# Ten norm stages of a hybrid transformer kernel, moved into the stages that use them

## The chip, the cores and the metric
The kernel runs on one core of a Trainium2 chip. The metric is the device time in microseconds of one execution: 2873.79 us, the median of three runs (2870.31 to 2880.94).

## The reference
Eight sub-layers, each of the form x = x + f(layernorm(x)), on x of [4, 256, 256] float32, which is 1024 tokens of 256 features. In order: linear attention, mixture of experts (8 experts, top 2), convolution with a scan, the same mixture of experts, softmax attention, a block "L1_ffn" of softmax attention and a routed FFN, delta-rule attention, and the L1_ffn block again.

```python
def _layernorm(x, axis=-1, eps=1e-05):
    m = jnp.mean(x, axis=axis, keepdims=True)
    v = jnp.var(x, axis=axis, keepdims=True)
    return (x - m) / jnp.sqrt(v + eps)
```

Some sub-layers put an RMS norm on top, x * rsqrt(mean(x*x) + eps) * weight: linear attention (eps 1.19e-7, no weight), convolution (1e-6, norm_scale) and the first half of L1_ffn (1e-6, w_ln1). The second half of L1_ffn starts with an RMS norm alone (w_ln2), on the residual inside the block. Convolution and L1_ffn keep the layer-normed x as their own residual, so it is added to the output besides x.

## The kernel before
Everything is hand-scheduled. X and XN are SBUF tensors of 128 partitions x 8 tiles x 256 features (token-major), XT is 128 x 2 x 1024 (feature-major, what the projections need). PS is the PSUM, eight banks of 512 float32. A `Stage` takes semaphores from a pool of 80 and opens SBUF tensors; inside an `nc.Block()` each engine has its own program, and order between engines is by semaphores alone. `Stage.end` clears the stage's semaphores on GpSimd and puts a barrier over all engines, after which the next stage starts with everything at zero. `Chain.then` makes an engine wait for its own last instruction.

`norm` (L163 to L258) is such a stage. VectorE does bn_stats on eight tiles, then bn_aggr on eight (mean and variance), ACT the square root (L236), VectorE the reciprocal (L200) and eight scalings (L202) of X into XN. With an RMS norm on top, VectorE works out its mean square from variance and rstd (L209, L210), ACT takes a second root (L239), VectorE a reciprocal (L218) and eight scalings into H (L220). Only when all eight tiles are scaled does TensorE transpose them (L255, 16 transposes into four banks); VectorE copies the banks of the first 128 features to XT (L227 or L230), ACT those of the second (L244 or L247), with the weight multiplied in where there is one. With `layer=False` (twice, ahead of the routed FFN) there is only the RMS norm, of XN.

`program` calls it ten times, each right ahead of the stage that needs XT: linear_attention (L261), moe (L404, twice), conv_scan (L694), softmax_attention (L926, three times), routed_ffn (L1285, twice) and delta_attention (L1574). In these stages SP issues the weight loads first; with the start of a stage TensorE waits for them. Beside that, at the start of a stage:
- moe: ACT copies XN twice into the row buffer XW (L591, L592), VectorE sets constants, TensorE runs the router (L513), 16 matmuls of 8 columns.
- conv_scan: GpSimd sets constants (L757 to L762), copies half heads of the weights when they have landed (L767, L768) and adds XN to X (L770). VectorE clips XT into XP (L775) and does four taps of a causal convolution in two halves (L786 and six of L788), then ACT takes the SiLU and TensorE starts (L904). VectorE goes on to the head_mix products KM (L797), which are wanted much later.
- softmax_attention: GpSimd sets V's zeros (L1011), the causal masks (L1012 to L1018), in the form with RoPE it swaps half heads (L1027, L1028), in the plain form it adds the output bias to X (L1032). VectorE makes a small table (L1207, L1209), ACT warms up Exp (L1152).
- routed_ffn: ACT rounds XT to XP (L1480), VectorE takes the remainder (L1538), TensorE runs the router (L1418).
- delta_attention: SP spills X and loads eleven sets of constants (L1645 to L1655), GpSimd sets six buffers, the last S with 8192 elements per partition (L1666), VectorE reorders XT into XB (L1686) and XP (L1690), TensorE multiplies XB (L1674), a barrier follows, then the loop over four blocks.

Of the kernel before, what the change touches and what calls it, by code (L numbers as in the profile page):

```python
# [10 lines left out]
ALU = mybir.AluOpType  # L11
# [151 lines left out]
def norm(core, layer=True, rms_eps=None, weight=None):  # L163


    nc, X, XN, XT, PS = core.nc, core.X, core.XN, core.XT, core.PS
    s = Stage(core, "norm")
    stats = s.sb("stats", [P, NT, 6])
    mv = s.sb("mv", [P, NT, 2])
    root = s.sb("root", [P, NT])  # L170
    rstd = s.sb("rstd", [P, NT])
    rms = s.sb("rms", [P, NT])
    eps = s.sb("eps", [P, 2])
    w = s.sb("w", [P, KD])
    H = s.sb("H", [P, NT, D]) if rms_eps is not None else XN
    w_in, sumsq, rooted, scaled, turned, moved, chain_v = (s.sem(n) for n in (
        "w_in", "sumsq", "rooted", "scaled", "turned", "moved", "chain_v"))
    src = X if layer else XN
    with nc.Block() as block:
        @block.sync  # L180
        def _(sp):
            if weight is not None:
                sp.dma_start(w[:], weight.rearrange("(k p) -> p k", p=P),
                             allow_slow_non_contiguous=True).then_inc(w_in, 16)
                sp.wait_ge(w_in, 16)

        @block.vector
        def _(dve):
            c = Chain(dve, chain_v)
            nc.vector.memset(eps[:, 0:1], LN_EPS)  # L190
            c.then(nc.vector.memset(eps[:, 1:2], rms_eps or 0.0))
            for i in range(NT):
                last = nc.vector.bn_stats(stats[:, i, :], src[:, i, :])
            c.then(last)
            for i in range(NT):
                last = nc.vector.bn_aggr(mv[:, i, :], stats[:, i, :])
            if layer:
                last.then_inc(sumsq, 1)
                dve.wait_ge(rooted, 1)
                c.then(nc.vector.reciprocal(rstd[:], root[:]))  # L200
                for i in range(NT):
                    last = nc.vector.tensor_scalar(XN[:, i, :], X[:, i, :], mv[:, i, 0:1], rstd[:, i:i + 1],  # L202
                                                   ALU.subtract, ALU.mult)
# [18 lines left out]
            for q in range(2):  # L222
                dve.wait_ge(turned, q + 1)
                if weight is not None:
                    if q == 0:
                        dve.wait_ge(w_in, 16)
# [2344 lines left out]
```

## Time and profile before

| what | us |
|---|---|
| median of three runs | 2873.79 |
| profiled execution, whole | 2874.2 |
| its span | 2872.4 |
| TensorE busy (matmuls) | 2101.9 (73%) |
| VectorE busy | 1594.2 (55%) |
| GpSimd busy | 1183.2 (41%) |
| ACT busy | 1119.7 (39%) |
| mean granted TensorE clock, of full speed | 0.817 |
| the transposes L255, per norm | 3.64 to 3.68 |
| router matmuls L513, 95.95 to 102.95 | 7.0 |
| last instruction before to first after a barrier: 79.41 to 80.07 (12 semaphores), 91.28 to 91.88 (7), 390.34 to 391.06 (24), 740.94 to 741.70 (30) | 0.66, 0.60, 0.72, 0.76 |
| GpSimd's opening work in plain attention, 605.76 to 610.16 | 4.4 |
| plain attention: transposes end 604.6, L1051 starts 608.6; granted clock 608.6 to 611.7 | 0.50 |
| first rotated key for ACT in attention with RoPE: 760.22 to 775.05 | 14.8 |

No engine is busy all the time, so a busy share alone says little here: the program is a row of stages, and in each another chain sets the length. Times in the rows below count from the start of the span. TensorE's matmul records are called PE, its weight loads PEld, VectorE DVE, GpSimd POOL, SyncE's DMA queue SPq.

### The profile page before, as it was taken

To read this page: it belongs to the slowest core of one execution; us is meant where nothing else is said; L and a number is where in the kernel's file an instruction comes from. 1 tells how busy PE (TensorE), PEld (TensorE's weight loads), DVE (VectorE), ACT (ScalarE), POOL (GpSimd) and SP (SyncE) were. 2 spreads that over 40 slices of the span, in tenths; PEclk is the share of its full clock that TensorE was granted. 3 is DMA by queue.
4 is the path that set the end of the run, shared out by engine and by line. 5 is a ranking of instruction groups with operands and counts; after the bars stand their busy time and mean duration, and the time that the engine had idled before them with its cause. 6 is when DMAs were issued, how large, how long until landed. Compare 5 with 4: busy or idle time off the path is not lost. (4 is left out here: it accounts for less than half of the span.)

```text
span 2872.4 us, 41835 instructions
## 1 busy us (share of the span) xinstructions
PE 2101.9 (73%) x15312; PEld 1628.4 (57%) x15312; DVE 1594.2 (55%) x3209; ACT 1119.7 (39%) x2681; POOL 1183.2 (41%) x999
## 2 busy tenths in 40 slices
PE   6398438958776995856797577965789667668698
PEld 4264224635354784746687466854667656435486
DVE  1322752234554334786876967867677678354433
ACT  2111221125254332743465444643446434215433
POOL 0222112210000652696736965378643869100154
PEclk9599668979898996967699586976779676879799
DMA  7232003210001502331323322233222422100250
GB/s 242 97 63 37 19 28 74 22 39 1 21 1 40 180 0 57 112 120 62 125 75 101 116 74 97 92 105 108 88 70 79 122 89 89 58 25 1 65 154 15
DMA packets 137424, 212.91 MB, mean 74 GB/s; under 512 B 61184, under 2 KB 113680, under 8 KB 132112
## 3 DMA queue, kind: packets, MB, share of 16 engines
q1 hardware_dynamic: 129072, 200.11, 21.7%
q0 software_dynamic: 8160, 10.26, 2.3%
q8 instruction: 118, 1.93, 0.3%
q14 instruction: 74, 0.61, 0.1%
HBM read 187.97 MB, written 22.37 MB: 73 GB/s over the span
## 5 line engine op out<-in xcount | busy, mean ns | idle before, releaser
L1977 PE MATMUL PS<-ident,XT 128*128 128x128 f32 x512 | 114.2, 405 | 251.6 <-DVE XT L2349 237.8
L2291 DVE SCALAR_TENSOR_TENSOR XT<-M_delta,CW_delta,XT 128x256 f32<-128x256 f32 x576 | 249.8, 494 | 71.4 <-ACT M_delta L2160 41.7
L1926 PE MATMUL PS<-XP_delta,X 128*128 128x268 f32 (+1 forms) x1024 | 241.4, 388 | 6.7 <-DMA X<-in_L_attn_b_heads 6.6
L1977 PEld LDWEIGHTS PS<-ident,XT 128*128 128x128 f32 x512 | 91.3, 209 | 271.1 <-DVE XT L2349 132.4
L1926 PEld LDWEIGHTS PS<-XP_delta,X 128*128 128x128 f32 x1024 | 192.9, 189 | 56.4 <-issue 11.9
L1439 PE MATMUL PS<-XP_rffn,UW_rffn 128*128 128x512 f32 x816 | 195.1, 396 | 5.8 <-POOL UW_rffn L1395 4.6
L1395 POOL TENSOR_TENSOR UW_rffn<-W_rffn,UW_rffn 128x512 fp32r<-128x512 f32 x34 | 44.2, 1299 | 347.4 <-ACT UW_rffn L1498 347.4
L1865 POOL TENSOR_TENSOR DD_delta<-DD_delta,A_delta 128x64 f32<-128x64 f32 (+6 forms) x224 | 170.0, 759 | 39.2 <-ACT A_delta L2248 19.5
L1439 PEld LDWEIGHTS PS<-XP_rffn,UW_rffn 128*128 128x128 f32 x816 | 155.9, 192 | 39.8 <-issue 7.1
L1891 POOL TENSOR_TENSOR M_delta<-M_delta,DD_delta 128x2304 f32<-128x2304 f32 x32 | 165.0, 5157 | 0.0
L505 POOL DMA_INDIRECT sums<-XS_moe,token_moe x46 | 71.7, 1559 | 219.0 <-ACT XS_moe L601 200.0
L1990 PEld LDWEIGHTS PS<-XN,KQ_delta 16*128 16x128 f32 (+2 forms) x3072 | 148.7, 295 | 7.3 <-issue 7.3
L2262 ACT ACTIVATE S_delta<-S_delta,AO_delta 128x128 f32<-128x128 f32 x512 | 152.1, 390 | 0.0
L1251 DVE TENSOR_REDUCE NM_attn<-PS 128x4 f32<-128x512 f32 (+1 forms) x144 | 92.1, 682 | 107.0 <-PE PS L1077 107.0
L1990 PE MATMUL PS<-XN,KQ_delta 16*128 16x16 f32 (+2 forms) x3072 | 151.3, 345 | 0.0
L1558 DVE TENSOR_TENSOR SU_rffn<-PS,CB_rffn 128x512 f32<-128x512 f32 x68 | 47.0, 691 | 181.3 <-PE PS L1439 158.6
L1957 PE MATMUL PS<-KQ_delta,TR_delta 128*128 128x64 f32 x1024 | 136.4, 280 | 14.6 <-DVE TR_delta L2308 14.5
L2240 ACT COPY KQ_delta<-PS 128x512 f32<-128x512 f32 x128 | 73.2, 584 | 179.0 <-PE PS L1977 179.0
L1957 PEld LDWEIGHTS PS<-KQ_delta,TR_delta 128*128 128x128 f32 x1024 | 131.3, 201 | 18.9 <-DVE TR_delta L2308 18.9
L1404 POOL TENSOR_TENSOR HP_rffn<-HF_rffn,HP_rffn 128x512 fp32r<-128x512 f32 x68 | 92.5, 1380 | 116.8 <-ACT HP_rffn L1521 116.8
L1175 ACT ACTIVATE PR_attn<-PS,NM_attn 128x256 f32<-128x256 f32 (+1 forms) x384 | 129.1, 466 | 28.1 <-DVE NM_attn L1251 28.1
L1807 POOL TENSOR_SCALAR XT<-M_delta,CW_delta,CB_delta 128x256 f32<-128x256 f32 x64 | 51.7, 808 | 163.1 <-ACT M_delta L2160 163.1
(359 smaller groups left out, 5038.6 us busy)
## 6 DMA issues: line engine op xcount, KB each, us to landing
M_delta<-gram_delta SPq DMA_DIRECT2D x32, 2304.0 KB, 8.8
X<-in_L_attn_b_heads SPq DMA_DIRECT2D x64, 512.0 KB, 3.2
EW<-in_L_ffn_w SPq DMA_DIRECT2D x24, 512.0 KB, 9.1
CB_rffn<-routes_rffn SPq DMA_DIRECT2D x20, 512.0 KB, 23.2
XN<-in_L_attn_b_outs SPq DMA_DIRECT2D x16, 512.0 KB, 3.6
F_delta<-in_L_attn_b_outs SPq DMA_DIRECT2D x4, 2048.0 KB, 8.2
W_rffn<-in_L_ffn_tiles SPq DMA_DIRECT2D x4, 1536.0 KB, 11.5
slots<-pad SPq DMA_DIRECT2D x2, 2967.0 KB, 14.5
```

The costliest lines, as they stand in the source:

```text
L1175: last = nc.scalar.activation(PR[:, u % (2 * ROWS), j * w:(j + 1) * w], PS[:, r, j * w:(j + 1) * w], ACT.Exp, bias=NM[:, u % (2 * ROWS), j ...
L1251: nc.vector.tensor_reduce(NM[:, u % (2 * ROWS), 0:per], PS[:, r, :].rearrange("p (h j) -> p h j", h=per), AX.X, ALU.max, negate=True).then ...
L1404: nc.gpsimd.tensor_tensor(HP[1][:, r, x], HF[:, n, :], HP[0][:, r, x], ALU.subtract).then_inc(hl_d, 1)
L1439: last = nc.tensor.matmul(PS[:, 4 + 2 * n + q, :], UW[qw][:, r, (q * KD + k) * P:(q * KD + k + 1) * P], XP[qx][:, k, n * NB:(n + 1) * NB], ...
L1865: last = nc.gpsimd.tensor_tensor(DD[:, :, tri(t - 1) + 1:tri(t)], DD[:, :, tri(t):tri(t + 1)], step(t).broadcast_to([P, BH, C - t]), ALU.mult)
L1891: nc.gpsimd.tensor_tensor(q, q, by_h(DD[:]), ALU.mult).then_inc(mq_d, 1)
L1926: last = nc.tensor.matmul(PS[:, 1 + i, 0:B * (WIN - halo)], WH[:, r, i, k, :], XP[:, k, :, n * BT + halo:n * BT + WIN], start=(k == 0), st ...
L1957: last = nc.tensor.matmul(PS[:, 5 * (g % 2), i * 2 * OC:(i + 1) * 2 * OC].rearrange("p (q t) -> p q t", q=2), TR[:, g % 3, i * P:(i + 1) * ...
L1977: last = nc.tensor.transpose(PS[:, 6 + r % 2, i * P:(i + 1) * P], W[:, B * h:B * (h + 1), :], core.ident[:])
L1990: last = nc.tensor.matmul(PS[:, 1 + b, h * 2 * C:(h + 1) * 2 * C].rearrange("p (q t) -> p q t", q=2), WT(o)[rows, h, :], GR[rows, o, h].re ...
L2262: last = nc.scalar.activation(S[:, lane, :], S[:, lane, :], ACT.Copy, scale=AO[:, lane:lane + 1])
L2291: nc.vector.scalar_tensor_tensor(TMP[:, r, i], RAW[:, r, i, :, tau:tau + BT], CW[:, i, h, tau:tau + 1], TMP[:, r, i], ALU.mult, ALU.add).t ...
```

## The change
The function `norm` goes. A class `Norm` takes its place; it has one method for each engine, which writes the norm's instructions at the head of that engine's program in the stage that uses it, with the stage's own semaphores. There is no barrier between norm and stage. `ready` and `rows_ready` are waits for XT and for the scaled rows, put where the stage reads them. SP's loads of the stage, GpSimd's opening work and the norm run beside each other.

Within the norm the tokens go in two halves of four tiles for the statistics, roots and scale factors. Even tiles are scaled by VectorE, odd ones by ACT (Identity with scale and shift, the shift being -mean * scale). The RMS norm's scale is 1/sqrt((1 + eps2) var + eps1 eps2), straight from the variance, so there is one scaling only; the plain layer norm that conv_scan and L1_ffn need as residual is made by eight more activations on ACT after the norm (`residual`). TensorE transposes tile by tile as they come.

```diff
-def norm(core, layer=True, rms_eps=None, weight=None):   # the whole stage goes
+class Norm:
+    def ready(self, engine):
+        engine.wait_ge(self.moved_v, 2)
+        engine.wait_ge(self.moved_a, 2)
+
+    def rows_ready(self, engine):
+        engine.wait_ge(self.tile_v, NT // 2)
+        engine.wait_ge(self.tile_a, NT // 2)
...
+    def vector(self, dve):
+        nc, mv, XT, PS = self.core.nc, self.mv, self.core.XT, self.core.PS
+        c = Chain(dve, self.chain)
...
+        for q in range(2):
+            h = self.half(q)
+            for i in range(h.start, h.stop):
+                last = nc.vector.bn_stats(self.stats[:, i, :], self.src[:, i, :])
+            c.then(last)
+            for i in range(h.start, h.stop):
+                last = nc.vector.bn_aggr(mv[:, i, :], self.stats[:, i, :])
+            if self.layer:
+                last.then_inc(self.stat_d, 1)
...
+        for q in range(2):
+            h = self.half(q)
+            dve.wait_ge(self.root_d, q + 1)
+            if self.layer:
+                c.then(nc.vector.reciprocal(self.scale[:, 0:1 + self.use, h], self.root[:, 0:1 + self.use, h]))
+                u = 1 + self.use
+                nc.vector.scalar_tensor_tensor(self.shift[:, 0:u, h], mv[:, h, 0].unsqueeze(1).broadcast_to([P, u, NT // 2]), -1.0,
+                                               self.scale[:, 0:u, h], ALU.mult, ALU.mult).then_inc(self.scale_d, 1)
...
+            for i in range(h.start, h.stop, 2):
+                if self.layer:
+                    nc.vector.tensor_scalar(self.H[:, i, :], self.src[:, i, :], mv[:, i, 0:1],
+                                            self.scale[:, self.use, i:i + 1], ALU.subtract,
+                                            ALU.mult).then_inc(self.tile_v, 1)
...
+        for q in range(2):
+            dve.wait_ge(self.turned, 2 * q + 1)
...
+                nc.vector.tensor_copy(XT[:, 0, q * NB:(q + 1) * NB], PS[:, q, :]).then_inc(self.moved_v, 1)
+
+    def scalar(self, act):
+        for q in range(2):
+            h = self.half(q)
+            act.wait_ge(self.stat_d, q + 1)
+            last = nc.scalar.activation(self.root[:, 0, h], mv[:, h, 1] if self.layer else self.square[:, h], ACT.Sqrt,
+                                        bias=self.eps[:, 0:1])
+            if self.use:
+                last = nc.scalar.activation(self.root[:, 1, h], mv[:, h, 1], ACT.Sqrt, bias=self.eps[:, 1:2],
+                                            scale=1.0 + self.rms_eps)
+            last.then_inc(self.root_d, 1)
+        for q in range(2):
+            h = self.half(q)
+            act.wait_ge(self.scale_d, q + 1)
+            for i in range(h.start + 1, h.stop, 2):
+                if self.layer:
+                    nc.scalar.activation(self.H[:, i, :], self.src[:, i, :], ACT.Identity, bias=self.shift[:, self.use, i:i + 1],
+                                         scale=self.scale[:, self.use, i:i + 1]).then_inc(self.tile_a, 1)
...
+    def tensor(self, pe):
+        for q in range(2):
+            h = self.half(q)
+            for i in range(h.start, h.stop):
+                if i % 2 == 0:
+                    pe.wait_ge(self.tile_v, i // 2 + 1)
+                else:
+                    pe.wait_ge(self.tile_a, i // 2 + 1)
+                for k in range(KD):
+                    last = nc.tensor.transpose(PS[:, 2 * k + q, (i - h.start) * P:(i - h.start + 1) * P],
+                                               self.H[:, i, k * P:(k + 1) * P], self.core.ident[:])
...
+    def residual(self, act):
+        for i in range(NT):
+            nc.scalar.activation(self.core.XN[:, i, :], self.src[:, i, :], ACT.Identity, bias=self.shift[:, 0, i:i + 1],
+                                 scale=self.scale[:, 0, i:i + 1]).then_inc(self.residual_d, 1)
```

In the stages (conv_scan shown; the others alike):

```diff
+    norm = Norm(core, s, rms_eps=1e-6, weight=a["L0_attn_b_norm_scale"],
+                hidden=GT[:].rearrange("p k n -> p (k n)").rearrange("p (i d) -> p i d", d=D))
         @block.sync
         def _(sp):
+            norm.sync(sp)
...
+            pool.wait_ge(norm.residual_d, NT)
             nc.gpsimd.tensor_tensor(X[:], X[:], XN[:], ALU.add).then_inc(res_d, 1)
         @block.vector
         def _(dve):
+            norm.vector(dve)
+            norm.ready(dve)
...
         @block.scalar
         def _(act):
+            norm.scalar(act)
+            norm.residual(act)
             act.wait_ge(c_in, 48)
...
         @block.tensor
         def _(pe):
+            norm.tensor(pe)
+            norm.ready(pe)
             pe.wait_ge(w_in, 64)
```

moe waits with `rows_ready` on ACT ahead of L591; routed_ffn with `ready` on ACT ahead of L1480; plain attention with `rows_ready` on GpSimd ahead of L1032; delta_attention with `ready` on VectorE ahead of L1686. With weights or a residual, H is laid over a buffer that the stage fills later (GT, PR or CB). `core.clear(6)` in delta_attention becomes the count of its semaphores; each stage has 11 more.

## Rows read from the trace of the kernel before

**Rows 1.** Windows: stretch, length, busy us of each engine, granted clock, DMA.
```profile
core 0: us, PE busy (x) PEld busy (x) DVE busy (x) ACT busy (x) POOL busy (x), PEclk, DMA share, GB/s
7.24:30.15 22.91, 3.68 (x17) 3.28 (x17) 10.34 (x38) 4.14 (x6) 0.00 (x0) 0.88 0.29 84
80.27:95.95 15.68, 3.67 (x17) 3.28 (x17) 8.74 (x66) 6.60 (x7) 0.97 (x5) 0.58 0.18 57
286.20:304.46 18.26, 3.67 (x16) 3.27 (x16) 13.36 (x39) 3.07 (x5) 3.20 (x6) 0.50 0.06 6
391.25:405.05 13.80, 3.68 (x16) 3.28 (x17) 8.74 (x66) 4.74 (x6) 0.97 (x5) 0.58 0.07 21
594.15:608.64 14.49, 3.68 (x17) 3.28 (x17) 9.37 (x29) 4.05 (x6) 2.82 (x3) 0.62 0.09 19
741.90:760.22 18.32, 3.64 (x16) 3.27 (x16) 12.20 (x40) 4.55 (x7) 3.38 (x5) 0.59 0.12 29
907.04:921.28 14.24, 3.68 (x17) 3.28 (x17) 8.43 (x38) 5.34 (x6) 0.00 (x0) 0.57 0.07 5
1089.32:1116.89 27.57, 3.68 (x16) 3.28 (x16) 19.48 (x32) 3.84 (x5) 11.24 (x6) 0.57 0.41 45
2519.66:2538.19 18.53, 3.67 (x16) 3.27 (x17) 12.21 (x40) 4.32 (x7) 3.57 (x5) 0.59 0.12 30
2688.36:2702.66 14.30, 3.68 (x16) 3.27 (x16) 8.48 (x38) 5.59 (x6) 0.00 (x0) 0.50 0.07 7
30.15:35.04 4.89, 4.89 (x6) 2.18 (x7) 0.00 (x0) 0.60 (x1) 0.00 (x0) 0.50 1.09 318
1125.00:2506.00 1381.00, 1018.31 (x9280) 882.37 (x9280) 1000.60 (x1916) 663.77 (x1716) 862.25 (x704) 0.77 0.28 93
```

**Rows 2.** Timeline, first norm: start, length, engine, line, instructions, idle before.
```profile
7.24 2.71 DVE L193 BATCH_NORM_STATS2 stats_norm<-X 128x6 f32<-128x256 f32 x8
...
10.66 0.30 ACT L236 ACTIVATE root_norm<-mv_norm,eps_norm 128x8 f32<-128x8 f32 x1 [2.34 <-DVE mv_norm L196]
...
11.23 2.67 DVE L202 TENSOR_SCALAR XN<-X,mv_norm,rstd_norm 128x256 f32<-128x256 f32 x8
...
17.16 3.67 PE L255 MATMUL PS<-ident,H_norm 128*128 128x128 f32 x16 [17.16 <-DVE H_norm L220]
...
20.87 0.58 ACT L247 COPY XT<-PS 128x512 f32<-128x512 f32 x1 [0.27 <-PE PS L255]
22.05 0.38 SPq L280 DMA_DIRECT2D W_linattn<-in_L_attn_a_Wq  x1
...
30.15 23.31 PE L291 MATMUL PS<-XT,W_linattn 128*128 128x512 f32 x48 [9.31 <-DMA W_linattn<-in_L_attn_a_Wp]
```

**Rows 3.** Groups of ACT instructions: busy, mean ns, idle before.
```profile
L601 ACT ACTIVATE XS_moe<-PS,XS_moe 128x256 f32<-128x256 f32 x46 | 21.8, 474 | 159.1 <-PE PS L570 159.1
...
L591 ACT COPY XW_moe<-XN 128x2048 f32<-128x2048 f32 x2 | 3.8, 1902 | 1.2 <-PEq L122 1.2
```

**Rows 4.** Timeline of the delta stage's opening.
```profile
1100.93 0.32 SPq L1645 DMA_DIRECT2D spill_delta<-X  x1
...
1104.70 7.46 POOL L1666 MEMSET S_delta<- 128x8192 f32 x1
```

**Rows 5.** Timeline of the convolution stage, VectorE, then GpSimd.
```profile
301.15 2.90 DVE L775 TENSOR_SCALAR XP_cscan<-XT 128x2048 f32<-128x2048 f32 x1 [2.27 <-PEq L122]
...
305.91 7.58 DVE L788 SCALAR_TENSOR_TENSOR A_cscan<-XP_cscan,CW_cscan,A_cscan 128x1024 f32<-128x1024 f32 x6
...
313.80 5.06 DVE L797 TENSOR_TENSOR KM_cscan<-HM_cscan,IM_cscan 128x256 f32<-128x256 f32 x2
...
301.17 1.80 POOL L758 MEMSET KEEP_cscan<- 128x2048 f32 x1
...
313.62 4.50 POOL L770 TENSOR_TENSOR X<-X,XN 128x2048 f32<-128x2048 f32 x1
```

**Rows 6.** Timeline of plain attention's opening, VectorE.
```profile
605.80 0.29 DVE L1207 TENSOR_REDUCE HALF_attn<-ident 128x2 f32<-128x128 f32 x1 [2.23 <-PEq L122]
```

More of the change, by code:

```diff
@@ L160, in finish @@
     s.end()
-def norm(core, layer=True, rms_eps=None, weight=None):
[L166 to L193, printed above, removed]
-            c.then(last)
[L195 to L203, printed above, removed]
-                if rms_eps is None:
-                    last.then_inc(scaled, 1)
-                else:
-                    c.then(last)
-                    c.then(nc.vector.tensor_tensor(rms[:], mv[:, :, 1], rstd[:], ALU.mult))
-                    nc.vector.tensor_tensor(rms[:], rms[:], rstd[:], ALU.mult).then_inc(sumsq, 1)
@@ L211, in _ @@
             else:
                 c.then(last)
-                c.then(nc.vector.tensor_tensor(rms[:], mv[:, :, 0], mv[:, :, 0], ALU.mult))
-                nc.vector.tensor_tensor(rms[:], rms[:], mv[:, :, 1], ALU.add).then_inc(sumsq, 1)
-            if rms_eps is not None:
-                dve.wait_ge(rooted, 1 + layer)
-                c.then(nc.vector.reciprocal(rms[:], root[:]))
-                for i in range(NT):
-                    last = nc.vector.tensor_scalar(H[:, i, :], XN[:, i, :], rms[:, i:i + 1], None, ALU.mult)
-                last.then_inc(scaled, 1)
@@ L249, in _ @@
-        @block.tensor
-        def _(pe):
-            pe.wait_ge(scaled, 1)
-            for k in range(KD):
-                for q in range(2):
-                    for i in range(4):
-                        last = nc.tensor.transpose(PS[:, 2 * k + q, i * P:(i + 1) * P],
-                                                   H[:, 4 * q + i, k * P:(k + 1) * P], core.ident[:])
-                    last.then_inc(turned, 1)
-    s.end()
+                c.then(nc.vector.tensor_tensor(self.square[:, h], mv[:, h, 0], mv[:, h, 0], ALU.mult))
@@ L509, in _ @@
         def _(pe):
+            norm.tensor(pe)
+            norm.ready(pe)
             pe.wait_ge(g_in, 16)
@@ L888, in _ @@
         def _(pe):
+            norm.tensor(pe)
+            norm.ready(pe)
             pe.wait_ge(w_in, 64)
@@ L1036, in _ @@
         def _(pe):
+            norm.tensor(pe)
+            norm.ready(pe)
             pe.wait_ge(q_in, QK_IN)
@@ L1328, in routed_ffn @@
         "up_mm", "silu_d", "su_d", "h_d", "dn_mm", "yt_ev", "y_mm"))
+    norm = Norm(core, s, layer=False, rms_eps=1e-6, weight=a["L1_ffn_w_ln2"],
+                hidden=CB[:, 0:2].rearrange("p m n -> p (m n)").rearrange("p (i d) -> p i d", d=D))
     PIECES = []
@@ L1414, in _ @@
         def _(pe):
+            norm.tensor(pe)
+            norm.ready(pe)
             pe.wait_ge(g_in, 32)
@@ L1479, in _ @@
         def _(act):
+            norm.scalar(act)
+            norm.ready(act)
             nc.scalar.copy(XP[0][:], XT[:]).then_inc(xh_d, 1)
@@ L1669, in _ @@
         def _(pe):
+            norm.tensor(pe)
+            norm.ready(pe)
             pe.wait_ge(c_in, CIN)
@@ L1684, in _ @@
         def _(dve):
+            norm.vector(dve)
+            norm.ready(dve)
             for k in range(KD):
```

116 lines of the change are left out of this document (83 added, 33 removed).

## The prediction
> **What bounds the kernel now.** I read the stretches between stages first, since the change lives only there. At ten places a norm stands as a stage of its own, closed by a barrier, and the stage behind it then starts its loads and waits for them. The windows table [rows 1] has one line for each place, cut from the norm's first bn_stats to the first instruction of the next stage that needs XT and a loaded operand (for the convolution stage: its first tap). The reader is to see that each stretch is 14 to 28 us long and that TensorE does one thing in it, the 16 transposes (3.6 to 3.7 us busy); the first ten lines add up to 178.1 us, 6.2% of the span. Nothing else of the program can run there, so whatever a stretch loses the whole time loses, as long as the stage behind it keeps its shape.
>
> The timeline of the first place [rows 2] shows what a stretch is made of: bn_stats of eight tiles 7.24 to 9.95, the square root on ACT at 10.66, eight scalings by VectorE 2.67, for norms followed by an RMS norm a second round until 17.16, transposes, and 20.87 + 0.58 = 21.45 the last copy. Only at 22.05 does SP issue the first weight load, and TensorE starts at 30.15, released by that DMA. The loads need none of the norm's results: 8.10 us of 22.9 are a wait that could lie beside the norm.
>
> **The new norm, step by step.** All times count from the first bn_stats, s. VectorE: bn_stats cost 2.71/8 = 0.34 each, so the first half ends at 1.42; the gap from the last bn_stats to the root (9.95 to 10.66) makes eight aggregations 0.7, so four 0.36. First half done 1.8, second 3.6. ACT takes the first root (0.30) beside the second half, the second at 3.64 to 3.94 (with an RMS norm two small activations, to 4.2: still before it is needed). VectorE reaches the reciprocal of the first half at 3.6, the shift at 3.83, and tile 0 at 3.9; a scaling is 2.67/8 = 0.33 apart with 0.4 for one, so tile 0 is ready at 4.3. ACT's tiles: the trace has no ACT scaling SBUF to SBUF of 256 elements. From below 1.90/8 = 0.24, an eighth of its 2048-element copy from SBUF [rows 3]; from above 0.474, a 256-element scaling with a pointer, though out of PSUM [rows 3]. I take the upper, as it has the size and the form: tile 1 at 4.5, tile 3 at 4.95. Second half: VectorE tiles 4 and 6 ready at 5.3 and 5.65, ACT's 5 and 7 at 5.5 and 6.0. TensorE needs 3.67/16 = 0.23 for a transpose [rows 2], so 16 of them from 4.35 on end later than every tile: it sets the end. From its start to the last copy's end it took 21.45 - 17.16 = 4.29 before, the last copy now behind the same sixteenth transpose. XT is whole at s + 8.65, +0.1 where a weight is multiplied in. Its ends: 7.9, with TensorE starting when the second half's statistics are there (3.6 + 4.29), and 14.2, the old chain. The second scaling round of the RMS norms is gone (its root comes from the variance), so these gain 5.6, the plain ones 2.35. In the two norms with layer=False the square and the sum stand in each half ahead of the root, four dependent small operations of 0.2: s + 9.4.
>
> **What waits behind it, place by place** (stretches from [rows 1]):
> - Linear attention, 22.91: loads issued at 7.04 instead of 22.05 land 8.10 later, at 15.1; XT is whole at 7.24 + 8.65 = 15.9. TensorE starts at 15.95: -14.2. The large loads of expert weights queue behind these on SP as before, only earlier.
> - MoE, 15.68 and 13.80: the router weights land within 4 us of issue and are there. Both start at s + 8.7: -7.0 and -5.1. ACT's two row copies, 3.8 us [rows 3], and a table load of 1.28 now start when TensorE starts the router; they used to start 4 us before it. The router matmuls take 7.0 us (table above), so they cover 5.1; with the cover gone it would cost up to 5 each. VectorE's memsets come behind the norm, 1.1 us, under the same cover.
> - Softmax attention, 14.49 (plain) and 18.32, 18.53 (RMS): s + 8.7 and s + 8.8, plus 0.3 for GpSimd (below): -5.5, -9.2, -9.4. The residual (eight more activations on ACT, at 0.474 3.8 us) and the Exp warm-up lie where ACT had no work for 14 us, until VectorE's first rotated key; GpSimd's bias add waits for the rows and b_in, long before its result is due.
> - Routed FFN, 14.24 and 14.30: s + 9.45: -4.8 and -4.85. ACT's cast of XT now starts with the router instead of 2.6 us before; the router covers it.
> - Delta stage, 27.57. Before, a spill of X and eleven constant loads went out from 1100.93 [rows 4] and TensorE started at 1116.89 [rows 1], released by the last of them: 15.96 after the first issue. Issued from 1089.1 they end at 1105.05. XT unhindered would be whole at 1098 and its two reorderings at 1099.5, so loads alone would give -11.8.
> - Convolution: VectorE's clip at 301.15 can start at 295.0. It took 2.90, of which 1.80 was a stall (below); alone 1.1. The first tap moves from 304.46 to 296.1: -8.4, before the next paragraph.
>
> **Where it collides: VectorE and GpSimd.** The stage's GpSimd work now runs beside the norm. [rows 5]: the clip and GpSimd's memset start together at 301.15 and 301.17; the memset takes 1.80 and the clip 2.90, though it has the memset's 2048 elements. Later GpSimd's add of 4.50 starts at 313.62, and a pair of VectorE tensor_tensor over 256 elements started at 313.80 takes 5.06. So they hold each other up, for a whole instruction.
> Consequence one, convolution: the add (L770) waits for the residual, ready about 8 x 0.35 after XT, at 298, when VectorE is among its six taps (7.58 for six, two SBUF operands each [rows 5]). Before, it started when they were over, and stalled only head_mix products that nobody was waiting for. Bounds: 0 (GpSimd never gets between two taps) and 4.5. I take 4.5, for the pair at 313.80 is the nearest row: -8.4 + 4.5 = -3.9.
> Consequence two, delta: the 7.46 memset [rows 4] starts 3.8 after GpSimd's first, at 1092.9, and ends at 1100.3; VectorE's first scaling is due at 1093.2. ACT's tiles 1 and 3 pass, the rest wait for it. XT is whole at 1104.9, reordered at 1106.4 (two copies of 1024 elements, 0.75 each as an estimate: half of the clip's 1.1 and 0.2 for a start): -10.3 instead of -11.8.
> Consequence three, attention: GpSimd's opening memsets and selects last 4.4 (table above), the first scaling is due at 4.1: +0.3 each, counted above. Bn_stats beside a memset is in no row. Bounds 0 and the whole of GpSimd's opening work, 2.8 to 3.6 per place [rows 1]; I take 0: the VectorE rows that stall read or write with both operands large, and a reduction of 128 elements beside GpSimd's memset of V took 0.29 [rows 6].
> The Trainium skill has a rule for it (SBUF — State Buffer, "Who interferes with whom"): the port pair is an exclusive lock held for the full instruction, taken by fp32 copies and tensor_scalar from SBUF to SBUF, and by instructions with two SBUF inputs only against a GpSimd operation that reads SBUF. The rows agree: the clip is the first kind, the products against the add the second. By it bn_stats is free beside a memset and both losses come about, 6.0 us together; without it the sum would be 80.2.
>
> **Sum:** 14.2 + 7.0 + 5.1 + 5.5 + 9.2 + 9.4 + 4.8 + 4.85 + 10.3 + 3.9 = 74.2 us. The semaphores to clear grow by 11 at a stage's end; the gaps at barriers are 0.6 to 0.8 with 7 to 30 of them to clear (table above), so 0.05 each, 0.5 in all, inside the rounding. The profiled execution took 2874.2 us (span 2872.4), 0.4 over the median of 2873.79, so the sum needs no scaling: **2874.2 - 74 = 2800 us**.
>
> **Rivals.**
> A, more than that: GpSimd slips in without stalling the taps (+4.5), delta is held by loads alone (+1.5), attention by nothing (+0.9), and TensorE, with less idle time ahead, leaves its half clock sooner. After the load wait it ran 4.89 us at a granted 0.50, 1.2 of 2.4 GHz [rows 1]; at full clock that is 2.4 less, in four stages with large matmuls up to 9.8; half of that is 4.9. Together 86: 2788. For it: idle time does fall. Against: in plain attention only 4 us lay between transposes and matmul, and TensorE still began at half clock for 3 us (table above).
> B, all VectorE work stalls beside GpSimd, bn_stats too: attention 2.8 + 3.4 + 3.6 less 0.9, convolution 1.8, delta 4 (its statistics begin when the memset has ended): 14.7 dearer, 2815. Against: the 0.29 of [rows 6].
> C, the norm gets no shorter, for hand-overs between three engines eat what the halves bring, and only barrier and loads are gained: 2.35 x 4 + 5.6 x 4 + 1.6 x 2 = 35 less gain, 2835. Against: TensorE, not the hand-overs, is last in my chain.
> D, slower than before: the loss is in the delta loop, 1381 us with a mean granted clock of 0.77 and TensorE busy for 1018 [rows 1]. If it is granted less there because the program before it leaves less idle time, TensorE's share grows with 0.77/clock; 74 us are given back at 0.718, the point from which it decides; at 0.71 it is 86: 2886. Against: 36 us of mostly waiting stay ahead of the loop.
>
> **Chances.** Forecast 0.52 (own range 2792 to 2808), A 0.2, B 0.15, C 0.08, D 0.03; 0.02 for others. The range goes from 2781, beyond A, to 2821, beyond B. 0.5%, 14 us, is what a measurement can tell from no change. All but D and a rest clear it: faster 0.95, same 0.02, slower 0.03.
>
> **What would show it.** After: the first transpose starts 4.3 to 4.5 after the first bn_stats, the last XT copy ends at s + 8.7; linear attention's first matmul at 15.9, released by a copy and not by a DMA; the GpSimd add inside the taps and one tap of about 5.7 instead of 1.28; in delta a scaling of 7 us. Wrong would be a table load between root and scaling, a router that waits for ACT, stages of another length behind these places, or a delta loop off 1381 us by more than 5.

## The result and the profile after

| | before | after |
|---|---|---|
| median, first chip (4 runs each) | 2877.03 us (2870.31 to 2880.94) | 2789.88 us (2775.62 to 2798.12) |
| ratio, 95% interval | | 0.9698 [0.9658, 0.9738] |
| the same kernels again, another chip (7 and 4 runs) | 2871.90 us | 2785.42 us, ratio 0.9708 [0.9677, 0.9738] |
| profiled execution, its span | 2874.2, 2872.4 | 2775.6, 2773.9 |
| mean granted TensorE clock in it | 0.817 | 0.831 |
| ACT busy, GpSimd busy | 1119.7, 1183.2 | 1156.1, 1181.7 |

The change gains 87 us; I had forecast 74 (2800 us). The time is 10 us under that, inside the wide range of 2781 to 2821, but below the 2792 to 2808 that I had given to the forecast itself, and nearest to rival A's 2788. The profiled execution of after is the fastest of its four, so the two profiles differ by 98.6 us and about 11 of these are the run. I therefore read five profiles of after's layout: the first, its repetition (again), add_late and s_split in the stages that they leave alone, and v_only, which changes the norm but has XT ready at after's times.

The windows of after, cut as in [rows 1]: from the first bn_stats of a stage to the first instruction that needs XT (in the third line, the convolution, to its first tap).

```profile
7.35:15.94 8.59, 3.67 (x17) 3.20 (x17) 6.66 (x26) 5.28 (x12) 0.00 (x0) 1.00 0.81 251
63.65:72.21 8.56, 3.67 (x16) 3.28 (x17) 6.81 (x46) 5.00 (x10) 0.78 (x5) 0.66 0.39 125
262.38:272.35 9.97, 3.67 (x16) 3.17 (x16) 8.02 (x28) 6.78 (x15) 3.96 (x9) 0.50 0.49 135
363.44:371.99 8.55, 3.67 (x16) 3.28 (x17) 6.80 (x46) 4.99 (x10) 0.77 (x5) 0.69 0.38 124
563.39:572.38 8.99, 3.68 (x17) 3.29 (x17) 7.22 (x27) 5.02 (x10) 6.62 (x7) 0.55 0.49 146
702.96:712.09 9.13, 3.68 (x17) 3.31 (x17) 7.53 (x28) 5.73 (x12) 6.24 (x14) 0.63 0.55 159
856.56:865.92 9.36, 3.68 (x17) 3.31 (x17) 7.15 (x36) 4.66 (x10) 0.00 (x0) 0.64 0.80 293
1029.08:1045.46 16.38, 3.68 (x17) 3.31 (x17) 14.41 (x30) 6.28 (x10) 9.44 (x5) 0.59 0.69 74
2438.26:2447.41 9.15, 3.68 (x17) 3.31 (x17) 7.55 (x28) 5.72 (x12) 6.26 (x14) 0.50 0.61 159
2596.87:2606.24 9.37, 3.68 (x17) 3.31 (x17) 7.15 (x36) 4.67 (x10) 0.00 (x0) 0.52 0.79 294
```

The stretches of 13.8 to 22.9 us have become 8.6 to 10.0, delta's 27.57 has become 16.38, and the DMA share, which stood at 0.06 to 0.29 in them, is 0.38 to 0.81: the loads run here now. In all ten TensorE still does only its 16 transposes, 3.7 us. (The granted clock of 1.00 in the first line is no reading: in this trace the clock's record starts only at 15.2 us, and the transposes took the 3.67 that they take in the third line at 0.50.)

Timeline of the first stretch (start, length, engine, line, instructions, idle before), the answer to [rows 2]:

```profile
7.15 0.38 SPq L329 DMA_DIRECT2D W_linattn<-in_L_attn_a_Wq  x1
...
11.08 0.73 DVE L239 TENSOR_SCALAR XN<-X,n_mv_linattn,n_scale_linattn 128x256 f32<-128x256 f32 x2
...
11.30 2.06 ACT L271 ACTIVATE XN<-X,n_shift_linattn,n_scale_linattn 128x256 f32<-128x256 f32 x4
...
11.54 3.67 PE L296 MATMUL PS<-ident,XN 128*128 128x128 f32 x16 [11.54 <-DVE XN L239]
...
15.25 0.59 ACT L284 COPY XT<-PS 128x512 f32<-128x512 f32 x1 [1.12 <-PE PS L296]
...
15.94 20.84 PE L342 MATMUL PS<-XT,W_linattn 128*128 128x512 f32 x48 [0.72 <-DVE XT L253]
```

The first load goes out at 7.15 instead of 22.05. The transposes start 4.19 us after the first bn_stats (7.35), XT is whole after 8.49, and TensorE is released by a copy at 15.94, where before it was released by a DMA at 30.15. The 48 matmuls then take 20.84 us; before they took 23.31.

The convolution stage, VectorE and then GpSimd, against [rows 5]:

```profile
271.09 1.23 DVE L841 TENSOR_SCALAR XP_cscan<-XT 128x2048 f32<-128x2048 f32 x1 [0.26 <-ACT XT L281]
...
272.35 1.42 DVE L852 TENSOR_SCALAR A_cscan<-XP_cscan,CW_cscan 128x1024 f32<-128x1024 f32 x2
...
273.80 11.80 DVE L854 SCALAR_TENSOR_TENSOR A_cscan<-XP_cscan,CW_cscan,A_cscan 128x1024 f32<-128x1024 f32 x6
...
274.99 4.50 POOL L834 TENSOR_TENSOR X<-X,XN 128x2048 f32<-128x2048 f32 x1 [2.53 <-ACT XN L305]
...
285.91 0.88 DVE L863 TENSOR_TENSOR KM_cscan<-HM_cscan,IM_cscan 128x256 f32<-128x256 f32 x2
```

The clip takes 1.23 instead of 2.90, the first tap comes 9.97 us after the first bn_stats instead of 18.26, and GpSimd's addition now starts among the six taps, which take 11.80 instead of 7.58: one of them, begun at 275.00, takes 5.56 where the others take 1.28. The pair of L863 is free of it (0.88 instead of 5.06).

The delta stage's opening, against [rows 4]:

```profile
1029.08 1.40 DVE L215 BATCH_NORM_STATS2 n_stats_delta<-X 128x6 f32<-128x256 f32 x4
1029.11 2.02 POOL L1757 MEMSET DD_delta<- 128x2304 f32 x1
...
1030.81 1.37 DVE L215 BATCH_NORM_STATS2 n_stats_delta<-X 128x6 f32<-128x256 f32 x4
...
1031.59 6.93 POOL L1759 MEMSET S_delta<- 128x8192 f32 x1
...
1032.77 6.20 DVE L239 TENSOR_SCALAR XN<-X,n_mv_delta,n_scale_delta 128x256 f32<-128x256 f32 x2
...
1045.46 6.49 PE L1769 MATMUL PS<-WB_delta,V_delta 128*128 128x16 f32 x32 [3.07 <-DMA LN_delta<-in_L_attn_b_ln_b]
...
1056.95 3.50 PE L2024 MATMUL PS<-XP_delta,X 128*128 128x268 f32 x7 [5.00 <-DMA X<-in_L_attn_b_heads]
```

Two scalings that take 0.73 us elsewhere take 6.20: the first takes 5.88 and ends at 1038.66, just behind the memset of S (1038.52), the second takes the usual 0.39. Bn_stats of four tiles takes 1.40 beside the memset of DD and 1.41 in the first stage, where GpSimd does nothing. The router is then released by the last small load, and the loop starts 27.87 us after the first bn_stats instead of 40.85.

### The profile page after: what moved, and what is told of

Same layout as the page of the kernel before. It is cut to its first block and busy times, and to the rows that moved or that the text cites. A ratio compares the mean times of both kernels' runs of the same rounds, so it can differ in the third digit from the quotient of the medians.

```text
span 2773.9 us, 41652 instructions
## 1 busy us (share of the span) xinstructions
PE 2081.8 (75%) x15312; PEld 1614.5 (58%) x15312; DVE 1565.3 (56%) x3155; ACT 1156.1 (42%) x2759; POOL 1181.7 (43%) x999
```

## The experiments

Every kernel ran four times and is compared with seven runs of before on the same chip. The rows with one time of before belong together; across them I compare ratios.

| kernel | median us | before there | ratio |
|---|---|---|---|
| own_stage | 2840.92 | 2873.49 | 0.9876 [0.9849, 0.9903] |
| one_chain | 2815.05 | 2873.49 | 0.9789 [0.9769, 0.9809] |
| add_late | 2779.24 | 2873.49 | 0.9670 [0.9654, 0.9686] |
| warm | 2774.95 | 2873.49 | 0.9655 [0.9635, 0.9675] |
| again (after) | 2785.42 | 2871.90 | 0.9708 [0.9677, 0.9738] |
| v_only | 2791.90 | 2871.90 | 0.9731 [0.9699, 0.9763] |
| s_split | 2788.83 | 2871.90 | 0.9710 [0.9691, 0.9729] |
| best | 2764.04 | 2871.90 | 0.9619 [0.9591, 0.9647] |
| pause | 2811.12 | 2879.42 | 0.9769 [0.9742, 0.9795] |
| one_chain_warm | 2794.30 | 2879.42 | 0.9706 [0.9681, 0.9730] |

### own_stage and one_chain: a shorter norm, or overlap?

```diff
 # own_stage: each stage, ahead of its own block
+    norm.alone()        # the new norm in a block of its own, then all_engine_barrier()
 # one_chain: the norm stays in the stage
-        return slice(q * NT // 2, (q + 1) * NT // 2)
+        return slice(0, NT)                    # one round of statistics, root, scale
-            for i in range(h.start, h.stop, 2):
+            for i in range(h.start, h.stop):   # VectorE scales all eight tiles, ACT none
+        pe.wait_ge(self.tile_v, NT)            # ahead of all transposes
```

> The new norm (two halves, VectorE and ACT four tiles each, one scaling instead of two) put back in front of each stage behind its own barrier, so that loads and GpSimd's opening work again start only after it. Theory (the gain has two parts, a shorter norm and loads that run beside it): the last XT copy ends 8.5 to 9.3 us after the first bn_stats in all ten stages, delta included (no memset runs beside it), where before had 11.0 (plain) and 14.3 (with RMS); that is 5.7 + 2.5 + 5.7 + 2.5 + 2.5 + 5.3 + 1.7 + 2.5 + 5.3 + 1.7 = 35 us under the kernel before, 2842, and each stage's first matmul waits for its last load again. Rival 1 (the split is not felt, all is overlap): 2875. Rival 2 (the norm is all): 2790.

> The norm stays inside its stage with the loads beside it, but as one chain: all eight bn_stats, one root, VectorE alone scales all eight tiles (one scaling, as in after), the transposes wait for all eight. Theory: last XT copy at 11.0 to 11.5 us instead of 8.5 to 9.3 in eight stages (+2.4 each = +19), convolution the same +2.4, delta: eight VectorE scalings behind the 6.93 us memset of S instead of four, but its loads end at 16.4 anyway, +0 to +2: 22 us over after, 2812. Rival (halves and the second engine are worth nothing once loads overlap): 2790.

Measured: 2840.9 (2842 expected) and 2815.1 (2812). First stage of own_stage, then of one_chain:

```profile
16.58 0.38 SPq L363 DMA_DIRECT2D W_linattn<-in_L_attn_a_Wq  x1
...
24.71 5.52 PE L376 MATMUL PS<-XT,W_linattn 128*128 128x512 f32 x8 [9.71 <-DMA W_linattn<-in_L_attn_a_Wp]
```

```profile
11.35 2.67 DVE L238 TENSOR_SCALAR XN<-X,n_mv_linattn,n_scale_linattn 128x256 f32<-128x256 f32 x8
14.07 3.68 PE L281 MATMUL PS<-ident,XN 128*128 128x128 f32 x16 [14.07 <-DVE XN L238]
...
18.47 22.69 PE L328 MATMUL PS<-XT,W_linattn 128*128 128x512 f32 x48 [0.72 <-DVE XT L252]
```

In own_stage XT is whole at 8.1 to 9.3 in all ten stages, as in after, but loads go out behind it and TensorE waits for a DMA again. The shorter norm alone gives 1.2%, 33 us; removing the barrier and letting loads run beside it gives the other 54. In one_chain XT comes at 11.0 to 11.5 (delta 16.0): its ratio of 0.9789 against 0.9698 puts 26 us of the 87 on what it leaves out: the halves, the second engine, and transposing tile by tile. The later starts alone sum to 23 us. Both rivals fall.

### v_only: is it the halves or the second engine?

```diff
-            for i in range(h.start, h.stop, 2):
+            for i in range(h.start, h.stop):   # halves stay; ACT's scaling loop is gone
-                if i % 2 == 0: ... tile_v ... else: ... tile_a ...
+                pe.wait_ge(self.tile_v, i + 1)
```

> Halves and loads beside the norm stay, but VectorE scales all eight tiles (0.36 us a tile), ScalarE none. Theory (the transposes set the pace: sixteen in 3.67 us, 0.46 a tile at half clock, slower than VectorE's 0.36): the last XT copy stays within 0.5 us of after's 8.5 to 9.3 in all but delta, so that ScalarE's half is worth 0 to 4 us in the whole, 2790 to 2794; what one_chain lost was the halves. In delta VectorE's four scalings behind the memset are 1.46 instead of 0.73 us, XT at 14.6. Rival (two engines are worth the half of one_chain's loss): XT at 9.8 or later, 2802.

Measured: 0.9731 against 0.9708 for after on the same chip, intervals overlapping. First stage:

```profile
11.04 1.38 DVE L238 TENSOR_SCALAR XN<-X,n_mv_linattn,n_scale_linattn 128x256 f32<-128x256 f32 x4
...
11.50 3.67 PE L282 MATMUL PS<-ident,XN 128*128 128x128 f32 x16 [11.50 <-DVE XN L238]
...
15.21 0.59 ACT L273 COPY XT<-PS 128x512 f32<-128x512 f32 x1 [1.12 <-PE PS L282]
```

XT is whole at 8.49, to the hundredth as in after. VectorE delivers a tile in 0.35 us and two transposes of it take 0.46, so TensorE is last with one engine or with two. In delta XT is at 13.94 in both kernels too, where I expected 14.6. So ACT's tiles carry nothing that this can measure.

What one_chain lost isn't the halves alone, though. It also makes TensorE wait for all eight tiles before the first transpose. In the first stage VectorE's first scaling starts 3.73 us after the first bn_stats in after and v_only (11.08 - 7.35, 11.04 - 7.31) and 4.32 in one_chain (11.35 - 7.03), so the halves bring 0.6 of the 2.85 us by which XT is earlier. The other 2.3 are transposes that run beside the scalings instead of behind them: a first tile ready 0.4 after 4.32 and 4.29 from the first transpose to the last copy would give XT at 9.0, against 11.34 measured. That is an estimate from these rows; no kernel here has the one chain with tile-by-tile transposes.

### add_late: GpSimd's addition among the taps

```diff
             pool.wait_ge(norm.residual_d, NT)
+            pool.wait_ge(conv_d, KD)
             nc.gpsimd.tensor_tensor(X[:], X[:], XN[:], ALU.add).then_inc(res_d, 1)
```

> In the convolution stage GpSimd's residual addition (4.50 us) waits for the last taps instead of for the residual tiles alone. Theory (it held one tap of VectorE): the eight taps in the trace go from 11.80 back to 7.6 us for the six, the stage of 101.06 us falls by 4.2 to about 96.9, and the addition then holds one of the pair of L863 multiplications, which is covered. Rival (the taps are slow for another reason, say ACT's residual tiles that read the same memory): taps stay at 11.8, no change. In the whole: 4 us under after, 2786, within the spread of runs. The other nine stages repeat after: the delta loop shows whether its 8 us less than before were the change or the run (theory: run; loop between the two, 1381 and 1373).

Taps, addition and the pair of multiplications behind it:

```profile
275.01 7.51 DVE L855 SCALAR_TENSOR_TENSOR A_cscan<-XP_cscan,CW_cscan,A_cscan 128x1024 f32<-128x1024 f32 x6
...
282.69 4.51 POOL L835 TENSOR_TENSOR X<-X,XN 128x2048 f32<-128x2048 f32 x1 [7.56 <-DVE A_cscan L855]
...
282.84 5.09 DVE L864 TENSOR_TENSOR KM_cscan<-HM_cscan,IM_cscan 128x256 f32<-128x256 f32 x2
```

The six taps fall from 11.80 to 7.51, the stage from 101.06 (after; 100.71 again) to 97.08, and the pair rises from 0.88 to 5.09: the stall has moved to where nobody waits. In this stage the theory holds in every number. The whole kernel doesn't fit as well: its ratio of 0.9670 is 0.28 to 0.38 points under after's (8 to 11 us) where I expected 4. After was timed on other chips; whether the rest is the chip or chance isn't known, but a difference of ratios between chips can evidently be off by some us.

### s_split: the memset of S in pieces

```diff
-            nc.gpsimd.memset(S[:], 0.0)
+            for i in range(0, BH, BH // 16):      # DD likewise in four
+                nc.gpsimd.memset(S[:, i:i + BH // 16], 0.0)
```

> Delta's memset of S (128x8192, 6.93 us) in 16 pieces of 0.43 us and that of DD (2.02) in four; nothing else. Theory 1 (GpSimd's memset holds VectorE's scaling for as long as one instruction lasts): the two scalings take at most 1.6 us instead of 6.20, the last XT copy ends 9 to 10 us after the first bn_stats instead of 13.9. Theory 2 (the small loads are late next: the last one landed at 16.4 in after's profile): the router matmuls still start at 14.5 to 16.5, the stage gains 0 to 1 us, the whole nothing. Rival for 1 (the lock lasts as long as GpSimd has work): 6 us again. Rival for 2 (the memset was last): router at 11, 4 to 5 us gained.

```profile
1041.20 10.22 POOL L1761 MEMSET S_delta<- 128x512 f32 x16
1042.30 1.11 DVE L239 TENSOR_SCALAR XN<-X,n_mv_delta,n_scale_delta 128x256 f32<-128x256 f32 x2
...
1046.16 0.69 DVE L253 COPY XT<-PS 128x512 f32<-128x512 f32 x1 [0.82 <-PE PS L296]
...
1054.17 6.98 PE L1771 MATMUL PS<-WB_delta,V_delta 128*128 128x16 f32 x32 [7.94 <-DMA LN_delta<-in_L_attn_b_ln_b]
```

Both theories hold: two scalings take 1.11 us instead of 6.20 and XT is whole at 8.25 instead of 13.93, so the hold lasts for one instruction; the router still starts at 15.57, released by the last small load, and the time is after's (0.9710 against 0.9708). The 6.9 us memset was a stall that cost nothing, since the loads end as late. In pieces it takes 10.22 us, and most of the increase is not the cutting: a piece takes 0.52 us beside bn_stats and beside copies out of PSUM, 0.67 beside the scalings, and 1.07 beside VectorE's reordering copies of 1024 elements, which themselves take 0.98 to 1.09 instead of 0.65. The two engines hold each other in turn.

### again: what was the run?

> The changed kernel unaltered, on the chip of the three kernels beside it: what repeats from run to run is the kernel, what does not is the run. Theory: the delta stage behind its router is 1401 to 1404 us as in the four kernels so far (before, own stage, one chain, late addition), not the 1392.8 of the first profile of after, which then owed 8 us of its 98.6 to the run; the second MoE stage may fall by 5 instead of 2.95 against before. Rival (the change shortens the loop itself): 1393 again. The whole 2784 to 2798.

Delta's loop, from its first matmul to the next stage's bn_stats, takes 1389.5 us in before, 1381.3 in the first profile of after and 1385.9 here; in the nine other experiments 1386.7 to 1396.6. The first profile's loop is the shortest of all, so most of its 8 us are the run. Counted from the router's first matmul to the next stage, as I expected it, delta takes 1402.8 in before, 1392.8 in the first profile and 1397.8 here, between the 1401 to 1404 of my theory and the 1393 of its rival; the other three of the layout take 1400.0 to 1403.1.

In the second MoE stage the five profiles gain 2.94 to 3.99, so my 5.1 was too much there. Its router starts 5.25 earlier as forecast. What is lost again is TensorE's clock at the first expert tile; that tile's matmuls, in before and then here:

```profile
446.10 2.88 PE L542 MATMUL PS<-EW,XK_moe 128*128 x4
448.81 1.88 PE L551 MATMUL PS<-EW,XK_moe 128*128 x4
```

```profile
412.68 3.62 PE L598 MATMUL PS<-EW,XK_moe 128*128 x4
416.09 2.46 PE L607 MATMUL PS<-EW,XK_moe 128*128 x4
```

A matmul takes 1.06 us at half clock and 0.59 at full clock. Before has three slow ones here, after's layout five or six, and they cost 1.3 us in again; behind them every expert tile keeps its distance from before's to the hundredth. Attention has such steps too: in again's plain attention 16 matmuls of L1154 (at 626.80) run at a granted 0.50 and take 2.09 us instead of 1.15, and from there on the stage is 1.6 us behind after's. So the clock also moves inside the stages, and not to the gain of a shorter opening.

### warm, pause and one_chain_warm: TensorE's clock at a stage's start

```diff
 # warm (9) and one_chain_warm (14), ahead of the transposes
+        for i in range(WARM):
+            nc.tensor.matmul(PS[:, 7, 0:P], self.core.ident[:], self.core.ident[:], start=True, stop=True)
 # pause, attention and routed FFN: SyncE sends two small DMAs in a row once XT is whole
+            pe.wait_ge(norm.paused, 32)           # ahead of the first matmul
```

> Nine 128x128 float32 matmuls of the identity into an unused bank ahead of each norm's transposes, where TensorE idles. Theory (the stage's first matmuls run at half clock where TensorE idled before them): the MoE routers fall from 6.96 to about 4.6 us, delta's from 6.49 to 4.5, the first four matmuls of the last attention from 3.75 to 1.9, routed FFN's 4.6 to 4.2; nine matmuls at half clock are 3.9 us, so that they end before the first scaled tile (4.2) and delay nothing. Sum 8 to 10 us under after: 2781. Rival 1 (the clock does not follow so little work): 2790. Rival 2 (what is gained is taken back by a lower granted clock in the body): routers shorter, total 2790.

> In the three softmax attentions and the two routed FFNs TensorE waits, between its transposes and its first matmul, for two small chained DMAs that SyncE starts once XT is whole (4 us of pure idle time; before had 2.8 to 4 there for its loads). Theory (TensorE's half clock at a stage's start follows from its idle time, and what the change gained beyond my sum is that this time went): these five stages start slow every time: 32 matmuls of plain attention 15.6 instead of 13.97 us, the first four of the other two 3.75, the routers 6.97 instead of 4.0 to 4.7. Each stage +4 for the pause and about 1.7 to 4 for the clock: 5 x 4 + 1.7 + 1 + 1 + 4 + 2 = 30 over after, 2817. Rival (whether the clock has risen is chance, the idle time does not bear on it): +20, 2808, with some starts fast.

> one_chain with 14 warming matmuls (5.9 us at half clock, before the first transpose at 6.8 to 7.1). one_chain's matmuls followed their transposes as closely as after's (0.72 us), yet its starts were slow in all but one stage (22.69, 6.97, 16.19, 3.75, 6.96, 3.75, 6.97). Theory (what counts is how long TensorE has idled before the transposes as well, 2.8 us more in one_chain): with that time filled the starts are fast (20.84, about 4.7, 13.97, 1.96, 4.4) and the transposes end sooner (last XT copy at 9.9 to 10.3 instead of 11.1 to 11.5): 10 stages x 1.1 + 10 for the clock = about 20 under one_chain, 2795. Rival (something else of one_chain keeps the clock down): transposes and starts as in one_chain, 2815.

Busy time in us of the first matmuls of each stage, by profile (the short value is the full clock, 2.4 GHz, the long one 1.2 GHz):

| profile | linear att. x48 | MoE routers x32 | plain att. x32 | att. x4, two stages | FFN routers x32 |
|---|---|---|---|---|---|
| before | 23.31 | 7.00, 7.00 | 15.62 | 3.78, 3.78 | 7.00, 6.99 |
| own_stage | 22.69 | 6.98, 6.97 | 16.63 | 3.75, 3.75 | 6.97, 6.83 |
| one_chain | 22.69 | 6.97, 4.69 | 16.19 | 3.75, 3.75 | 6.96, 6.97 |
| after | 20.84 | 6.96, 6.97 | 13.97 | 1.95, 3.75 | 4.62, 4.19 |
| again | 20.84 | 6.97, 6.96 | 13.97 | 3.75, 3.75 | 4.41, 4.69 |
| v_only | 20.84 | 6.96, 6.96 | 13.97 | 3.70, 1.96 | 6.97, 4.31 |
| s_split | 20.84 | 6.97, 6.97 | 13.97 | 3.75, 1.96 | 4.34, 4.54 |
| add_late | 22.57 | 6.97, 6.96 | 15.82 | 1.96, 1.96 | 3.98, 4.74 |
| pause (idle only from plain att. on) | 20.84 | 6.97, 6.96 | 15.67 | 3.75, 2.87 | 6.92, 6.93 |
| warm | 20.84 | 6.96, 3.91 | 13.97 | 1.95, 1.95 | 4.26, 4.07 |
| one_chain_warm | 20.84 | 4.77, 6.97 | 13.97 | 1.96, 1.96 | 4.81, 5.03 |
| best (warm as well) | 20.84 | 4.72, 6.97 | 13.97 | 1.95, 1.95 | 5.07, 4.22 |

TensorE in the second MoE stage of warm (the nine warming matmuls, which leave two records each as the routers' do, transposes, router), the same router at half clock in after, and two starts of pause:

```profile
361.65 2.25 PE L290 MATMUL PS<-ident 128*128 128x128 f32 x18 [1.28 <-PEq L123]
365.97 2.22 PE L299 MATMUL PS<-ident,XN 128*128 128x128 f32 x16 [2.07 <-DVE XN L240]
368.91 3.91 PE L572 MATMUL PS<-WG_moe,XT 128*128 128x8 f32 x32 [0.72 <-DVE XT L254]
```

```profile
371.99 6.97 PE L569 MATMUL PS<-WG_moe,XT 128*128 128x8 f32 x32 [0.72 <-DVE XT L253]
```

```profile
574.97 15.67 PE L1138 MATMUL PS<-XT,W_attn 128*128 128x512 f32 x32 [3.15 <-DMA pause_attn<-ident]
...
878.76 6.92 PE L1519 MATMUL PS<-WG_rffn,XT 128*128 128x9 f32 x32 [3.23 <-DMA pause_rffn<-ident]
```

Warm works and through one thing more than I expected: in seven of ten stages the transposes too run faster (2.2 to 2.9 us instead of 3.67), and XT is whole at 7.0 to 7.8. Its ratio is 0.43 to 0.53 points under after's, 12 to 15 us, but these are other chips. Add_late ran on warm's own chip: warm is 4.3 us under it and their intervals overlap; with the 4.2 that add_late gains in its stage this makes 8.5 us, as much as I had expected (8 to 10). So warming is worth 8 to 15 us. Pause: the two chained DMAs put 2.35 us in front of each of five matmuls, 12 us, not 20; its ratio is 0.61 to 0.71 points over after's, 18 to 20 us, and four of its five starts are wholly slow, the fifth at 2.87 in between. One_chain_warm stands 0.83 points under one_chain, 24 us, with XT at 9.3 to 9.8 instead of 11.0 to 11.5 in eight stages and all but one start fast. So time in which TensorE idles before a stage, wherever it lies, makes a slow start likelier, and work in its place a fast one. It isn't certain in either direction: the same layout gave both in the two long attentions, and the MoE routers are slow in all five profiles of after's layout, and once each in warm and in best behind transposes that had already run faster (2.85 and 2.84). What tips a single start is open.

### best: what the runs point to

```diff
 # add_late, warm (9) and s_split together; and in delta:
+            sp.dma_start(WB[:], ...).then_inc(b_in, 16)   # first of the loads
-            pe.wait_ge(c_in, CIN)
+            pe.wait_ge(b_in, 16)                          # the router waits for Wb alone
+            dve.wait_ge(c_in, CIN)                        # VectorE waits for the others, behind the router
```

> The late addition and the nine warming matmuls together, delta's memsets in pieces, and delta's Wb loaded first on a semaphore of its own, for which alone the router waits. Theory: the gains add: 4.2 (convolution), about 10 (clock, run to run between 5 and 12) and in delta the router starts at 11 instead of 15.5 to 16.4 and ends at 18, behind the last load: 4 to 5. Sum 18 to 20 under after: 2770. Rival 1 (warming and late addition draw on the same spread between runs): 2778. Rival 2 (delta's stage ends with its loads and heads' descriptors, not with the router): 2774.

```profile
1028.78 6.61 PE L1775 MATMUL PS<-WB_delta,V_delta 128*128 128x16 f32 x32 [2.72 <-DVE V_delta L1790]
...
1041.41 2.15 PE L2031 MATMUL PS<-XP_delta,X 128*128 128x268 f32 x4 [6.01 <-DMA X<-in_L_attn_b_heads]
```

2764.0 us (2770 expected), 21 under after on the same chip and clear of it by the intervals. The router of delta starts 10.50 us after the first bn_stats and the loop after 23.13 (after 27.87, again 27.33): once the loads are out of the way, the split memset should pay, for with the memset whole XT came only at 13.9; no kernel here loads Wb first with the memset whole, so this is argued. The convolution stage takes 95.38.

## Why the prediction was right, and where its sizes were off

Change of each stage in us, from first bn_stats to first bn_stats (the last one to the end of the span), against the one profile of before. In the convolution and in delta one of the five is left out, because its experiment changes that stage:

| stage | forecast | start of the first dependent instruction | whole stage, first profile | whole stage, mean of five profiles |
|---|---|---|---|---|
| linear attention | -14.2 | -14.32 | -16.73 | -16.45 |
| MoE | -7.0 | -7.12 | -7.20 | -7.16 |
| convolution | -3.9 | -8.29 + 4.22 | -3.99 | -4.09 (four) |
| MoE | -5.1 | -5.25 | -2.94 | -3.57 |
| plain attention | -5.5 | -5.50 | -8.18 | -5.42 |
| attention | -9.2 | -9.19 | -11.54 | -8.72 |
| routed FFN | -4.8 | -4.88 | -9.76 | -8.51 |
| delta | -10.3 | -11.19 | -21.15 | -16.6 (four) |
| attention | -9.4 | -9.38 | -10.09 | -13.32 |
| routed FFN | -4.85 | -4.93 | -7.04 | -6.57 |

- The openings. The second column sums to -75.8 against my -74.2, and every term but delta's is within 0.2 of its forecast. The norm did what the chain said: first transpose at 4.2 to 4.9, XT at 8.5 in MoE and linear attention (forecast 8.65), 8.9 in plain attention (8.95), 8.6 to 9.05 in the norms with RMS and a weight (8.75 to 9.05), 9.3 with layer=False (9.4). Only delta's first transpose is late, at 9.6. ACT's scaling, which no row of before had, takes 0.51 apiece (2.06 for four) against the 0.474 taken.
- The convolution. The addition held a tap for 4.2 us (5.56 for that tap, 5.7 forecast); add_late gave exactly that back.
- Attention. The 0.3 came, but not by the step that I named. VectorE's scaling took its usual 0.72 for two; what GpSimd's selects held was the shift ahead of it (L232, a small scalar_tensor_tensor), 0.59 us in plain attention and 0.56 with RMS, against 0.16 to 0.17 in delta and the convolution.
- Delta. The memset held VectorE's scaling as forecast (5.88 us where I had 7), but XT came at 13.9 instead of 15.6: S's memset began 2.5 us after the first bn_stats instead of 3.6, since the small memsets ahead of it took less time (DD 2.02 instead of 2.53, DC 0.58 instead of 1.12), and took 6.93 itself instead of 7.46. The router started at 15.5 to 16.4 instead of 17.3, and rival A's remark that the loads would hold delta by themselves was right (s_split). After it the loop's first matmul came another 1.1 to 1.8 sooner, with its own load.
- The clock was the mis-sized term. I put it at nothing in the sum and at 4.9 in rival A, because before's plain attention had begun slowly with only 4 us between transposes and matmul. With that gap gone it began fast in four of five profiles, as did linear attention; the FFN routers fell from 7.0 to 4.0 to 4.7 in nine of ten cases. In linear attention this is 2.5 us, in plain attention 1.65, in an FFN router 2.3 to 3.0. Medians say 87, openings 76: most of the 11 between them I give to the clock. Pause took it away again and warm added to it, which shows that idle time ahead of a start costs clock. How the 11 us divide is argued, not shown: the stages as wholes don't follow their starts (plain attention's first matmuls end 7.2 us earlier in four profiles of five, its stage gains 5.4 in the mean), because the clock also moves inside them, and part of delta's 16.6 is its loop, whose length differs by 10 us among the five profiles. What stands firm is the sum of the openings, 75.8 for 74.2; the whole gained 13 us more than I had forecast.
- The rivals. A forecast 2788 and is nearest in time, but two of its four reasons fail: GpSimd did hold a tap, and attention's 0.3 for GpSimd's selects is there (XT at 8.9 instead of 8.5, by the shift). Its reason on the clock, idle time that falls, is what the starts show. B fails on bn_stats, 1.40 beside a memset and 1.41 without. C fails: the norm got shorter by all that it had to. D fails: the loop was granted 0.76 to 0.77, before 0.77, and it takes 1381.3 to 1391.1 us in the five profiles, before 1389.5.

## What to carry to other kernels

Sum openings from a table that runs from "inputs there" to "first instruction that needs them"; such a sum held here to 2% for the openings, while the whole kernel gained 13 us more. A stage boundary costs three things, the barrier, the loads behind it and the half clock after idle time. The third went only with the others: without barrier and loads but with 2.8 us more of idle time (one_chain) nearly all starts stayed slow. Where TensorE must idle, a few matmuls of no use to anyone ahead of its next work bought 8 to 15 us. Before a second engine is given half of a job, ask whether the stage behind the job keeps up: here the transposes were slower than one engine's scaling, so a second engine brought nothing. What shortened the norm was to hand tiles over one by one (some 2.3 us a stage, by the estimate above) and, less, to halve the batch (0.6).

## What the runs showed of the hardware

- A GpSimd memset held VectorE's fp32 scaling from SBUF to SBUF until it ended, 6.20 us for two scalings beside a 6.93 us memset; in pieces of 512 elements it let them through (1.11 us). The hold goes both ways: a piece took 0.52 us alone, 0.67 beside scalings and 1.07 beside copies of 1024 elements, 10.22 in sum. That is the Trainium skill's rule that I used in the prediction (SBUF — State Buffer, "Who interferes with whom"), and add_late and s_split agree with it.
- The small shift with two SBUF operands (L232) took 0.16 us beside the memset of S, which reads nothing, and 0.59 beside the affine_select, which reads SBUF.
- Bn_stats, and copies out of PSUM, were not held: 1.40 us for four tiles beside a memset and 1.41 without; the last XT copy took 0.69 beside S's pieces and 0.69 without.
- Sixteen transposes take 3.67 us at half clock; behind nine matmuls they took 2.2 to 2.9 in seven of ten stages, behind fourteen (one_chain_warm) 1.97 in eight. The Trainium skill (TensorE: Matmul & The Clock Gate, "Part 4: PE-mode transpose") says that the full clock doesn't engage in transpose mode; these rows show transposes that run at it (granted clock 1.00 at 365.97 in warm), and matmuls 0.72 us behind them that start at it, in after's first stage with nothing but the 16 transposes ahead of them. That the number of slow matmuls differs from run to run of one kernel, as the Trainium skill says on the same page (Part 1: The HAM clock gate), the table of starts bears out.
